# Attention layer 1: three steps reordered on the DMA-issuing queue, one on ScalarE

## What is computed

```python
def multilora(x, W, A, B):              # one low-rank adapter per batch entry
    return x @ W.T + (x @ A.T) @ B.T
Q, K, V = multilora(x, Wq, Aq, Bq), multilora(x, Wk, Ak, Bk), multilora(x, Wv, Av, Bv)
Q, K = rope(Q), rope(K)                 # 16 heads of 32
attn = softmax(causal(Q @ K.T / sqrt(32)))
x = layernorm(x + multilora(attn @ V, Wo, Ao, Bo))
x = layernorm(x + ffn(x))               # a second attention inside, then a gated MLP of 2048
```

## Time and profile before

| what | value |
|---|---|
| three runs | 2896.36, 2898.29, 2898.55 us, median 2898.29 |
| the profiled execution | 2896.08 us, its span 2894.2 us |
| PE, busy share of the span | 92% |
| DVE, ACT, POOL | 55%, 46%, 22% |
| layer 1, 75 to 818 us: PE busy | 675.56 of 743 us |
| second attention, 818 to 1700 us: PE busy | 793.25 of 882 us |
| MLP, 1700 to 2894 us: PE busy | 1137.08 of 1194 us |

### The profile page before, as it was taken

One profiled execution on the slowest core, in us unless ns is written; L12 is line 12 of the kernel. 1 busy time (PEld: TensorE's weight loads), 2 busy tenths in 40 slices (PEclk: granted clock), 3 DMA queues, 4 the chain that ended last, 5 costly groups with the idle time before them and its releaser, 6 DMA issues. The chain is left out here.

```text
span 2894.2 us, 40922 instructions
## 1 busy us (share of the span) xinstructions
PE 2648.9 (92%) x13584; PEld 2025.0 (70%) x13584; DVE 1578.3 (55%) x4310; ACT 1335.0 (46%) x2755; POOL 645.4 (22%) x528
## 2 busy tenths in 40 slices
PE   5999999999758999999999984999999999999998
PEld 4777767777536666667667643888888888888886
DVE  4777777777635777887787763322222333333333
ACT  2777777777633666666666663211111221111111
POOL 5455555555321122222212111000000000000000
PEclk8999999999878999999999987999999999999999
DMA  5455655555635555545555434211111221111100
GB/s 141 97 138 137 138 126 137 133 133 122 152 85 126 121 102 142 119 103 131 120 120 117 107 65 151 78 46 45 45 45 47 92 76 46 47 45 45 45 29 29
DMA packets 173898, 276.44 MB, mean 96 GB/s; under 512 B 29204, under 2 KB 53524, under 8 KB 173076
## 3 DMA queue, kind: packets, MB, share of 16 engines
q1 hardware_dynamic: 170772, 260.58, 37.3%
q0 software_dynamic: 2304, 12.58, 1.3%
q10 hardware_dynamic: 640, 1.05, 0.1%
HBM read 97.04 MB, written 42.99 MB: 48 GB/s over the span
## 5 line engine op out<-in xcount | busy, mean ns | idle before, releaser
L2277 DVE TENSOR_TENSOR c_product<-c_up_ps,c_gate 128x512 f32<-128x512 f32 x128 | 88.5, 692 | 652.8 <-PE c_up_ps L2343 652.8
L2331 PE MATMUL c_gate_ps<-c_h_split,c_w_split 128*128 128x512 f32 x1536 | 380.1, 396 | 24.2 <-DVE c_w_split L2229 24.2
L2315 PE MATMUL c_down_ps<-c_w_split,c_product_split 128*128 128x512 f32 x1536 | 379.3, 396 | 0.0
L2343 PE MATMUL c_up_ps<-c_h_split,c_w_split 128*128 128x512 f32 x1536 | 378.2, 395 | 0.0
L2331 PEld LDWEIGHTS c_gate_ps<-c_h_split,c_w_split 128*128 128x128 f32 x1536 | 289.4, 188 | 95.9 <-issue 26.0
L2343 PEld LDWEIGHTS c_up_ps<-c_h_split,c_w_split 128*128 128x128 f32 x1536 | 288.3, 188 | 70.1
L2315 PEld LDWEIGHTS c_down_ps<-c_w_split,c_product_split 128*128 128x128 f32 x1536 | 288.8, 188 | 68.7
L2201 ACT ACTIVATE c_gate<-c_gate_ps 128x512 f32<-128x512 f32 x128 | 76.4, 597 | 492.4 <-PE c_gate_ps L2338 492.4
L287 DVE TENSOR_TENSOR a_prob_lo<-a_scores_t_ps,a_prob_hi 128x384 fp32r<-128x384 f32 (+1 forms) x384 | 225.4, 593 | 137.0 <-ACT a_scores_t_ps L280 135.3
L279 ACT ACTIVATE b_prob_hi<-b_scores_t_ps 128x384 fp32r<-128x384 f32 (+1 forms) x384 | 199.8, 520 | 211.5 <-PE b_scores_t_ps L270 190.8
L287 DVE TENSOR_TENSOR b_prob_lo<-b_scores_t_ps,b_prob_hi 128x384 fp32r<-128x384 f32 (+1 forms) x384 | 226.4, 593 | 122.6 <-ACT b_scores_t_ps L280 121.6
(11 more groups left out here) (206 smaller groups left out, 4776.4 us busy)
## 6 DMA issues: line engine op xcount, KB each, us to landing
a_q_stack<-a_q_split SPq DMA_DIRECT2D x192, 128.0 KB, 3.7
a_k_stack<-a_k_split SPq DMA_DIRECT2D x192, 128.0 KB, 3.7
b_q_stack<-b_q_split SPq DMA_DIRECT2D x192, 128.0 KB, 3.3
b_k_stack<-b_k_split SPq DMA_DIRECT2D x192, 128.0 KB, 3.7
c_h_stage<-h_t SPq DMA_DIRECT2D x16, 1024.0 KB, 6.2
c_res<-x SPq DMA_DIRECT2D x16, 1024.0 KB, 5.5
c_w_stage<-in_mlp_w POOLq DMA_DIRECT2D x16, 768.0 KB, 4.6
stage<-in_x_t SPq DMA_DIRECT2D x8, 1024.0 KB, 6.4
```

The source lines that it names most:

```text
L2277: dve.tensor_tensor(product[:, bank, :], up_ps[:, bank, :], gate[:, bank, :], ALU.mult).then_inc(product_done, 1)
L2315: mm = pe.matmul(down_ps[:, t, :], product_split[:, kt % 2, a, t * P:t * P + P], w_split[:, w, kt, 2 * KC * P:], start=(kt == 0 and i == 0 ...
L2331: pe.matmul(gate_ps[:, bank, :], w_split[:, w, ft, c * 2 * P:c * 2 * P + P], h_split[run.pair][:, a, c, :], start=(c == 0 and w == 0 and a ...
L2343: mm = pe.matmul(up_ps[:, bank, :], w_split[:, w, ft, c * 2 * P + P:(c + 1) * 2 * P], h_split[run.pair][:, a, c, :], start=(c == 0 and w = ...
```

## The change

In SP's step `send_b` moves ahead of `gather`, `load` moves behind `gather`, and `send_low` moves from ahead of `spread_out` to between `spread_out` and `spread_in`. In ACT's step `projected` moves ahead of the rounding of x chunks 2 and 3 and ahead of `low`. The first step of all, (0, 0), and the last batch have none of the moved calls except `gather`.

```diff
@@ SP
             def step(b, g):
                 last = is_last(b)
+                first = isinstance(b, int) and b == 0 and g == 0
+                if g == 1 and not last:
+                    send_b(b + 1)
+                if not first:
+                    gather(*group(b, g, -1))
                 if g == 0 and not last:
                     load(b + 1)
-                first = isinstance(b, int) and b == 0 and g == 0
                 if not first:
-                    gather(*group(b, g, -1))
+                    spread_out(*group(b, g, -1))
                 if g == 1 and not last:
-                    send_b(b + 1)
                     send_low(b + 1)
                 if not first:
-                    spread_out(*group(b, g, -1))
                     spread_in(*group(b, g, -1))
@@ ACT
+                    for tile in leaving(b, g, slot):
+                        projected(*tile)
                     if g == 1 and slot == 0 and not last:
                         for c in range(2, KC):
                             x_chunk(b + 1, c)
                     if g == 1 and slot == LOW_SLOTS[1] and not last:
                         low(b + 1)
-                    for tile in leaving(b, g, slot):
-                        projected(*tile)
```

## The result

The changed kernel takes 2871.62 us in the median of 4 runs (2864.92 to 2873.81) against 2897.32 us of the kernel before (4 runs, the three of above and one more), a ratio of 0.9908 with a 95% interval of 0.989 to 0.9926: 25.7 us less where 15.8 were forecast, and 1.4 us outside the range. A second set of six runs beside the kernel before, on another occasion, gave 0.9916 (0.9895 to 0.9937). The profiled execution took 2873.81 us, its span 2871.9 us, 22.3 less than that of before.

What follows compares the result with a forecast made beforehand. PE was taken as the bound, the engine the others wait on. Terms -12.1 - 3.0 + 0.7 - 1.1 + 1.1 + 0.7 - 3.6 + 1.5 = -15.8 us gave a 2882.5 us median; range 2873 to 2892.

Steps and rivals of the forecast that it cites:

- Part 4: Steps (b, 0), b = 1 to 6: load behind gather cuts ACT's idle time, down to an 18.4 us floor, -3.6 us.
- Part 5: Steps (b, 1), slot 8: PE stands 1.7 us, and one clock fall is booked, +1.5 us (between 0 and 10.5).
- Part 3: B's layout ahead of gather, 7 times: gather issued later, +1.1 us, and its sums landing later, +0.7 us.
- Part 1: Slot 1, steps (b, 2): sums sent before low-rank rows end seven holds, -12.1 us, two clock falls, -3.0; cost +0.7.
- Part 2: Slot 1 of steps (b, 1): bank emptied ahead of rounding; shorter hold waited for again, except batch 0, -1.1 us.

Runs made afterwards that it cites:

- the second experiment: Only the low-rank rows' send moved behind that of the inverse sums, against the kernel before: 0.9955, 2881.37 us.
- the pair of parts: Low-rank rows' send behind that of the inverse sums and ACT's bank emptying ahead of rounding, against the kernel before: 0.9936, 2879.53 us.

## Why the prediction was wrong, point by point

The direction and most mechanisms were right. The sum was 10 us short, and the first four terms below make most of that up.

**Part 4, load behind gather: -3.6 forecast, -7.7 measured. This is the step that failed most.** "With less idle time the slope ends: the shortest of the six is 18.4" took a floor from one step, (4, 0), and from a wrong reading of it. That step held a wait on a k stack besides, of which I took off the 0.40 us that the trace gives and not the 0.69 that PE was late by. Read rightly it was 18.1 us at 1.59 us of idle time and on the same line as the others, so nothing showed where the line ends. Moving load alone put all six at 17.8. The other profiles bear the line out: with load ahead of gather, in six kernels, 32 of the 36 steps take 16.54 us and ACT's idle time on top, within 0.05 us, the shortest 18.1 us at 1.58 us of idle time (the other four take 0.3 to 0.7 us more). With load behind gather every one of these steps takes 17.8 us. The two lines meet at 1.26 us of idle time; that is an estimate, as no step lies near it.

**Part 5, a fall of the clock at slot 8: +1.5 forecast, 0 measured**, in both profiles. And its premise failed: PE doesn't stand 1.7 us at slot 8. The wait there is 0.73 us in step (1, 1), as before. Of the returned 1.0 us of that step 0.2 is gone at slot 4, 0.3 more at slot 7 and 0.4 at slot 8, and the waits that the profile names there are smaller than that.

**Part 3, B's layout: +1.8 forecast, about 0 measured.** B didn't hold gather, but for 0.3 us once in the second profile of the changed kernel (in step (1, 1) of the first the queue was done with B at 188.33 + 1.85 = 190.18, and gather starts at 190.80): its issue took 1.85 us ahead of gather, and not the 2.63 that it took behind it. Nor did the sums land later: 5.35 us after gather's first issue in the mean of the seven steps, 5.3 before. The row that the forecast leaned on was misread besides: the 4.0 us of the earlier trace rows are the median over all steps, while the DMA of the sums in the six steps behind the 1 MB of load landed after 4.0 to 6.3 us, 4.4 in the median. There it took 5.9 us from gather's first issue in the mean, and 5.2 in the changed kernel, with load behind. The Trainium skill (page "DMA: Bandwidth & Descriptors", section on queues, rings and completion order) says that descriptors are consumed in ring order on each DMA engine. No delay from that shows for B's three DMAs; the later landing behind the 1 MB of load would fit it.

**Part 1, the holds: -12.1 and -3.0 forecast, -16.9 measured.** The holds ended in all seven batches, and both falls behind them with them. That there were two is a matter of the one profile: with the holds in place other kernels had none, one or three, behind holds of 1.71 to 2.41 us, so the reading that a stand of over 2 us makes the fall was too simple. What was missing is 1.8 us: PE is late by about 0.25 us more than each hold that the profile names (steps (b, 2) without a fall moved by 2.0, 1.4, 1.9, 1.9 and 1.9 us where the holds are 1.8, 1.1, 1.6, 1.7 and 1.6; the 0.40 us of step (4, 0) made 0.69 in part 4). Its cost, a longer wait on the low-rank rows, was +1.5 us in the changed kernel where I had 0.7; with part 1 alone it was 0.05, so most of it comes with the other parts, which bring PE there earlier.

**Part 2, the bank: -1.1 forecast for batch 0, -0.6 measured there, for an incomplete reason.** The other six batches gave 1.0 us together up to slot 8, which no term had. That ACT's copy in slot 5 gives the 1.0 us back was right, and moving the copy shows it. What the prediction didn't have is that the hold also carries falls of the clock, and that these depend on the rest: one or two of seven in the three profiles that have the holds on pair 0 as well, six of seven once the sums go out early, four of seven in the full change without this part. Part by part from the kernel before, the bank edit is worth 0; inside the change it is worth 3.5 us in the one pair of traces, and 3.8 between the second experiment and the pair of parts. The prediction booked the falls behind the removed holds and left those behind the hold that it called worthless.

The parts alone give -6.4, -13.0, -0.9 and -2.0 us (ratios times 2897), 22.3 together, and the whole 24.3 to 26.7. The difference is in the direction of the clock but inside the intervals.

What stays open: why the falls are so many when the sums go out early. The hold in front is the same 1.2 us in the trace of the kernel with one fall and in that with six. Each count is from one profiled execution, so how far it changes from one execution of a kernel to the next isn't known either. The last batch gives back 1 us of layer 1 in the profile after, and another 2 us are lost behind it against the profile of before; with executions that differ by 10 us I can't tell this from chance.

## What to carry to other kernels

Idle time of an engine that isn't the bottleneck costs nothing only until it stands in front of work that the bottleneck needs: measure the distance between two fixed instructions of the busiest engine in several repetitions and plot it against that idle time. If the points lie on a line of slope one, don't put the floor at the lowest of them: it may lie anywhere below (here 17.8 us and not 18.4). And a short hold of PE isn't worthless because its time is waited for again later; count the falls of the clock behind it, in more than one profile, and take into account that another edit can change their number. Where several DMAs make up one transfer, measure from the issue of the first to the landing of the last: the landing time of one of them changes when the issue of its neighbour does.

## What the runs showed that I hadn't expected

- A hold of PE of 1.2 us, with 0.74 us shortly before it, is followed by the clock at 0.50 in one, two, four or six batches of seven, depending on the kernel, at the same length of hold. Behind the holds on pair 0 it fell in none to three batches of seven: behind one of 1.71 us, and not behind one of 1.93.
- A fall makes its step 0.9 to 1.6 us longer up to slot 8, and 0.5 us in batch 0 of the changed kernel with the bank behind rounding. The kernel with parts 1 and 2 and the full change, which have neither hold, had no fall in these seven batches.
- Steps (b, 0), from slot 11 of the step before to slot 8, take 16.54 us and the time for which ACT stands idle at slot 5's copy, or 17.8 us, whichever is longer, in 80 of 84 steps over fourteen profiles, within 0.06 us.
- Gathered sums land 5.9 us after gather's first issue where a 1 MB DMA was issued ahead of gather, against 5.2 us in the changed kernel, with that DMA behind it (5.6 us where load alone moved). Three DMAs of 96 KB ahead of gather cost nothing that shows (5.3 and 5.35 us).
